# Gate logits of a routed feed-forward network: multiplied on TensorE instead of reduced on VectorE, and the instruction list written anew

## What is computed

```
x = x + (segment_sum(layernorm(x)[src] * edge_weight, dst) @ W.T + b)     # GNN
z = layernorm(x)
gates = softmax(z @ gW + gb)                   # gW is 256 x 4, gb has 4 numbers
topv, topi = top_k(gates, 2);  topw = softmax(topv)
x = x + mlp_shared(z) + sum over the 2 chosen experts of topw * mlp_expert(z)
```

## Time and profile before

| what | value |
|---|---|
| median of 3 runs | 400.21 us (397.77, 400.21, 401.97) |
| profiled execution: its own time | 397.88 us |
| its span, first to last instruction | 395.8 us |
| TensorE busy | 356.3 us (90%) |
| VectorE busy | 279.5 us (71%) |
| GpSimd busy | 277.5 us (70%) |
| ScalarE busy | 202.2 us (51%) |

### The profile page before, as it was taken

How to read it: one execution, slowest core, us unless ns; L and a number is a source line. 1 busy time by engine, 2 the same in 40 slices (tenths; PEclk the granted TensorE clock), 3 DMA queues, 4 the chain that set the end, 5 groups by cost and what they waited for, 6 DMA issues and landing times.

```text
span 395.8 us, 8049 instructions
## 1 busy us (share of the span) xinstructions
PE 356.3 (90%) x2319; PEld 284.6 (72%) x2319; DVE 279.5 (71%) x1199; ACT 202.2 (51%) x551; POOL 277.5 (70%) x294
## 2 busy tenths in 40 slices
PE   5996669989869999999999999999978999998773
PEld 3785568767768788877787877787866777766562
DVE  6598999692998999628899677662199522777371
ACT  2566796482487997023959953222085321243330
POOL 7777777777777777777777777777777777776000
PEclk9999879999989999999999999999999999999999
DMA  6999549844444554434343434343433344334000
GB/s 205 375 367 339 149 101 310 223 104 108 102 107 100 122 135 98 110 107 131 102 130 104 129 102 134 104 125 104 134 95 107 106 134 133 105 100 130 14 15 25
DMA packets 53857, 53.69 MB, mean 136 GB/s; under 512 B 32522, under 2 KB 43508, under 8 KB 53684
## 3 DMA queue, kind: packets, MB, share of 16 engines
q0 software_dynamic: 13536, 36.98, 31.3%
q1 hardware_dynamic: 35220, 10.53, 11.5%
q10 hardware_dynamic: 5056, 5.64, 4.1%
HBM read 46.64 MB, written 6.48 MB: 134 GB/s over the span
## 4 chain that ended last, share of the span: by engine, by line
PE 64%; DVE 11%; SPq 10%; issue 6%; DMA 4%; ACT 3%; DVEq 0%; ACTq 0%
PE agg_ps L1220 15%; PE hid_ps L1252 14%; SPq L739 7%; PE window_ps L1153 7%; PE tok_ps L1301 5%; DMA x_sb<-in_x 4%; PE agg_ps L1189 4%; PE build_ps L1207 3%; PE hid_ps L1265 3%; PE tok_ps L1299 3%; PE hid_ps L1261 3%; DVE gate_x L1678 3%; DVE high_node L1620 2%; PE agg_ps L1207 2%; ACT h L1006 1%
## 5 line engine op out<-in xcount | busy, mean ns | idle before, releaser
L832 POOL DMA_INDIRECT rows<-normalised_rows,src_all x246 | 239.8, 975 | 75.0 <-issue 75.0
L1220 PE MATMUL agg_ps<-xn_all,dense 128*128 128x256 f32 x350 | 79.7, 381 | 0.0
L1252 PE MATMUL hid_ps<-xt,pack 128*128 128x256 f32 (+2 forms) x336 | 70.6, 356 | 5.2 <-ACT xt L987 4.9
L1220 PEld LDWEIGHTS agg_ps<-xn_all,dense 128*128 128x128 f32 x350 | 65.3, 190 | 9.6 <-ACT dense L968 0.7
L1252 PEld LDWEIGHTS hid_ps<-xt,pack 128*128 128x128 f32 x336 | 56.0, 190 | 14.8 <-issue 8.0
L918 ACT ACTIVATE low_1h<-iota,lo_f 128x128 f32<-128x128 f32 x182 | 57.5, 393 | 0.6 <-ACT xn_all L904 0.4
L1006 ACT ACTIVATE h<-hid_ps,pack 128x256 f32<-128x256 f32 (+2 forms) x84 | 32.8, 442 | 41.4 <-PE hid_ps L1252 41.3
L1620 DVE TENSOR_SCALAR high_node<-iota,hi_f,own_w 128x125 f32<-128x125 f32 x182 | 50.6, 355 | 1.9 <-PE agg_ps L1207 1.6
L816 POOL DMA_INDIRECT rows<-in_x,src_first x36 | 35.3, 981 | 11.0 <-issue 10.4
L1678 DVE CUSTOM_DVE_ANT_0 gate_x<-xn,shared 128x256 f32<-128x256 f32 x100 | 41.9, 480 | 0.3
L1153 PE MATMUL window_ps<-rows,select 128*32 128x256 f32 x564 | 36.1, 384 | 1.7 <-DVE select L1570 1.7
(11 more groups left out here) (171 smaller groups left out, 525.5 us busy)
## 6 DMA issues: line engine op xcount, KB each, us to landing
rows<-normalised_rows,src_all POOLq DMA_INDIRECT x246
x_sb<-in_x SPq DMA_DIRECT2D x6, 512.0 KB, 10.3
normalised_rows<-xn_all ACTq DMA_DIRECT2D x6, 512.0 KB
records<-in_rec SPq DMA_DIRECT2D x184, 1.5 KB
out<-y SPq DMA_DIRECT2D x10, 256.0 KB
dense<-in_x_cols ACTq DMA_DIRECT2D x4, 512.0 KB, 8.9
pack<-in_packed SPq DMA_DIRECT2D x1, 1540.5 KB, 9.4
x_sb<-in_x SPq DMA_DIRECT2D x3, 256.0 KB, 10.7
```

The costliest lines, as they stand in the source:

```text
L832: pool.indirect_dma_start(rows[:, b % RING * BATCH + pos, :], None, table[:, :], bass.IndirectOffsetOnAxis(ap=src_all[:, c:c + 1], axis=0) ...
L1220: last = pe.matmul(dense_ps[0:r, t * D:(t + 1) * D], dense[:, h, t * P:t * P + r], xn_all[:, h, :], start=(h == 0 and t == 0), stop=(h == ...
L1252: last = pe.matmul(by_half(u.hid_ps[b % 2])[:, m % 2, 0:tok], w, u.xt[:, k, 0:tok], start=(k == 0), stop=(k == KD - 1))
```

## The change

The four logits of a tile are now two matmuls (one per half of the 256 features), with the transposed rows `xt` as the stationary operand and `gate_w_sb`, 128 x 4 per half, as the moving one, into the last eight columns of the bank `mid_ps`. The new step is `gated` (`gate_products`), after `xt`. `route` begins with a new `tensor_tensor` that adds the bias and writes `logit`, and waits for `gated` instead of for the 4 reductions a tile. `gates`, `gate_x` and its semaphore are gone; `norm` no longer waits for the reductions of the unit before. The gate weights move from the broadcast tile `shared` (1284 columns, now 260) to `pack` (8 columns more).

The list is made anew: the rank tables have other numbers, the head of the plan begins about 1 us later, `bias` of dense units may not be listed before 77.5 in the planner's clock (66.0 before), G8 comes before D3, and every TensorE duration is raised by 1.2%.

```diff
-UNIT_ORDER = "G0 D0 G1 G2 D1 G3 G4 G5 D2 G6 G7 D3 G8 G9"
+UNIT_ORDER = "G0 D0 G1 G2 D1 G3 G4 G5 D2 G6 G7 G8 D3 G9"
...
-COLD_AFTER, COLD = 1.9, 3.5
+COLD_AFTER, COLD, LATELY, ISSUE = 2.2, 4.0, 4.5, 1.012
...
-            ("dve", "bias", 0.07 + 0.265 * T, lambda: needs(66.0, prior("bias", one))),
+            ("dve", "bias", 0.07 + 0.265 * T, lambda: needs(66.0 if u.kind == "G" else 77.5, prior("bias", one))),
...
-            ("dve", "norm", 0.33 * T, lambda: needs(of("std"), prior("turn", one), prior("gates", one))),
+            ("dve", "norm", 0.33 * T, lambda: needs(of("std"), prior("turn", one))),
...
+            ("pe", "gated", 0.24 * T, lambda: needs(of("xt"))),
...
-            ("dve", "gates", 1.63 * T, lambda: needs(of("norm"))),
-            ("dve", "route", 0.29, lambda: needs(of("gates"))),
+            ("dve", "route", 0.45, lambda: needs(of("gated"))),
...
+        logit_ps = u.mid_ps[:, 512 - 2 * E:512].rearrange("p (t e) -> p t e", t=2)
...
+            def gate_products(q):
+                if q == 0:
+                    pe.wait_ge(s_w, 16)
+                pe.wait_ge(s["xt"], q + 1)
+                for t in range(UNITS[q].T):
+                    for k in range(KD):
+                        last = pe.matmul(logit_ps[:, t, :], u.xt[:, k, t * P:(t + 1) * P], gate_w_sb[:, k, :],
+                                         start=(k == 0), stop=(k == KD - 1))
+                last.then_inc(s["gated"], 1)
...
-                    dve.wait_ge(s_gate_x, E * sum(other.T for other in UNITS[:q]))
...
-            def gates(q):
-                done = E * sum(other.T for other in UNITS[:q])
-                dve.wait_ge(s["xn"], q + 1)
-                for t in range(UNITS[q].T):
-                    for e in range(E):
-                        if done >= 2:
-                            dve.wait_ge(s_gate_x, done - 1)
-                        dve.tensor_tensor_reduce(
-                            out=gate_x[:, done % 2, :], in0=u.xn[:, t, :], in1=gate_w_sb[:, e, :], scale=1.0,
-                            scalar=gate_b_sb[:, e:e + 1], op0=ALU.mult, op1=ALU.add,
-                            accum_out=u.logit[:, t, e:e + 1]).then_inc(s_gate_x, 1)
-                        done += 1
...
-                dve.wait_ge(s_gate_x, E * sum(other.T for other in UNITS[:n]))
+                dve.wait_ge(s["gated"], n)
+                dve.tensor_tensor(u.logit[R], logit_ps[R], gate_b_sb.unsqueeze(1).to_broadcast([P, T, E]),
+                                  ALU.add).then_inc(s["top"], 1)
+                dve.wait_ge(s["top"], 2 * q + 1)
```

More of the change, by code:

```diff
@@ L165 @@
 STATS_BEHIND = 3
-UNIT_ORDER = "G0 D0 G1 G2 D1 G3 G4 G5 D2 G6 G7 D3 G8 G9"
-RANKS = {"open": 3, "near": 0.021, "behind": 0.82, "dve_behind": 0.6, "act_behind": 0.83, "hurry": -0.87,
-         "batch": 2.09, "rawturn": 7.95, "rawlin": -3.57, "merge": 3.07, "windows": 10.79, "built": 1.07,
-         "rowstd": 3.76, "rawxt": 4.1, "rawout": -0.66, "low": 15.13, "select": -5.08, "select_late": 8.52,
-         "place": -10.1, "records": 4.9, "onehot": 1.04, "rowstats": 3.84, "rowshifts": -2.07}
-BUILD_RANKS = (4.56, 6.32, 2.65, -9.43)
-MULT_RANKS = (0.84, -9.23, 11.58, 11.51)
+UNIT_ORDER = "G0 D0 G1 G2 D1 G3 G4 G5 D2 G6 G7 G8 D3 G9"
+RANKS = {"open": 3, "near": 0.105, "behind": 0.46, "dve_behind": 0.83, "act_behind": 1.65, "hurry": -2.49,
+         "batch": 5.25, "rawturn": 14.77, "rawlin": -17.2, "merge": 7.43, "windows": 19.55, "built": 0.44,
+         "rowstd": 15.95, "rawxt": -2.24, "rawout": 12.98, "low": 22.59, "select": 3.55,
+         "select_late": -1.3, "place": -20.25, "records": 11.53, "onehot": -3.9, "rowstats": 5.81,
+         "rowshifts": -8.25}
+BUILD_RANKS = (2.58, 16.22, -1.26, -10.69)
+MULT_RANKS = (-5.54, -8.91, 10.79, 17.88)
 GATHER_US = 1.256
-COLD_AFTER, COLD = 1.9, 3.5
+COLD_AFTER, COLD, LATELY, ISSUE = 2.2, 4.0, 4.5, 1.012
 def schedule():
     lag = {"pe": 0.25, "act": 0.16, "dve": 0.16, "sp": 2.0}
-    free = {"pe": 35.5, "act": 43.9, "dve": 45.2, "sp": 64.2}
+    free = {"pe": 36.6, "act": 44.9, "dve": 46.2, "sp": 65.0}
     order = {e: [] for e in free}
-    cold = 0.0
-    done, units, left = {("load", 0): 31.0, ("load", 1): 46.0, ("load", 2): 58.5, ("load", 3): 61.5, ("records", 0): 35.0,
-            ("select", 0): 44.9, ("place", 0): 45.1}, [], {}
+    cold, idle = 0.0, []
+    done, units, left = {("load", 0): 31.0, ("load", 1): 46.0, ("load", 2): 59.5, ("load", 3): 62.5, ("records", 0): 36.0,
+            ("select", 0): 46.0, ("place", 0): 46.2}, [], {}
     done.update({("begin", v): 28.5 for v in range(1, len(DENSE))})
-    done.update({("onehot", k): 36.3 + 1.1 * k for k in range(EARLY)})
-    done.update({("low", k): 38.2 + 1.9 * k for k in range(EARLY)})
+    done.update({("onehot", k): 37.4 + 1.1 * k for k in range(EARLY)})
+    done.update({("low", k): 39.3 + 1.9 * k for k in range(EARLY)})
     open_units = []
@@ L396, in schedule @@
         if engine == "pe":
-            if begin - free["pe"] > COLD_AFTER:
+            idle.append((begin, begin - free["pe"]))
+            if sum(gap for to, gap in idle[-12:] if to > begin - LATELY) > COLD_AFTER:
                 cold = begin + COLD
+            took *= ISSUE
             took += min(took, max(0.0, cold - begin) / 2)
@@ L519, in build @@
         owner = sb("owner", [P, E, P // 2], BF16)
-        gate_x = sb("gate_x", [P, 2, D])
         u = WorkingSet()
@@ L661, in build @@
         steps_of_unit = (
-            "x1 stats var std rstd xn turned xt top low ex total inv gate gtop "
+            "x1 stats var std rstd xn turned xt gated top low ex total inv gate gtop "
             "ahead tied tied_before glow gex order rank kept ktotal kinv parts mix_turned mixt "
@@ L742, in load_weights @@
             def load_weights():
-                sp.dma_start(shared[:, :], every.to_broadcast([P, D + E * D + E])).then_inc(s_linear, 16)
+                sp.dma_start(shared[:, :], every.to_broadcast([P, D + E])).then_inc(s_linear, 16)
                 sp.dma_start(pack[:, :], packed).then_inc(s_w, 16)
@@ L1321, in _ @@
                         turn(q)
+                    elif name == "gated":
+                        gate_products(q)
                     elif name == "l1a":
@@ L1844, in _ @@
                         normalise(q)
-                    elif name == "gates":
-                        gates(q)
                     elif name == "route":
@@ L1917 @@
         np.asarray(L0_ffn_sW1).reshape(KD, P, D).transpose(1, 0, 2), ew1, b1,
-        np.asarray(L0_ffn_sW2).reshape(KD, P, P).transpose(1, 0, 2), ew2, b2, L0_ffn_sW3, ew3, b3_laid)], axis=1)
-    every = np.concatenate([row(L0_gnn_b), row(np.asarray(L0_ffn_gW).T), row(L0_ffn_gb)], axis=1)
+        np.asarray(L0_ffn_sW2).reshape(KD, P, P).transpose(1, 0, 2), ew2, b2, L0_ffn_sW3, ew3, b3_laid,
+        np.asarray(L0_ffn_gW).reshape(KD, P, E).transpose(1, 0, 2))], axis=1)
+    every = np.concatenate([row(L0_gnn_b), row(L0_ffn_gb)], axis=1)
     laid = [x, np.asarray(x).T, *chunks(src), *chunks(dst), *chunks(nxt), *chunks(edge_weight), rec,
```

12 lines of the change are left out of this document (6 added, 6 removed).

## The result

The kernel after the change takes 397.06 us (median of 20 executions, 394.80 to 400.25), the kernel before, run on the same chip in turns with it, 400.50 us (20 executions, 396.80 to 404.32). The ratio is 0.9934, with a 95% interval of 0.9910 to 0.9959: 0.7% faster, and the forecast of 401.1 lies 4 us too high, on the wrong side of no change; the range began at 397.5.

A forecast was written before the change was run, and what follows sets the result against it. TensorE's backlog was taken to set the end, the gathers 0.9 us behind as next bound. Terms -0.2 - 0.3 + 1.4 = +0.9 gave 398.8 on the profiled execution, 401.1 on the median's scale; range 397.5 to 405.5.

The forecast's parts named there:

- the sum: Whole kernel: -0.2 - 0.3 + 1.4 = +0.9 us, 398.8 on the profiled execution, 401.1 on the median's scale.
- The products: Gate matmuls on TensorE: 0.10 us a record, 0.40 a tile, 10.0 us for 25 tiles (8.0 to 12.2).
- From G7's `turn` to batch 23: TensorE's stretch up to the last batch: 27.6 us before, less 1.95 of first layer, plus 1.6 of gating, 27.25.
- Batch 23 to the merge: From the start of batch 23 to the merge's start: 2.46 us instead of 2.73, behind `l1b`.
- G9's `l1a` behind the merge's end: Serial tail: G9's first layer starts 6.8 us after the merge instead of 5.0, +1.8, of which gating is 0.8.
- Its first layer: G9's `l1a` to `l1c` in the tail: ScalarE's relu no longer waits behind `ex` for the logits, -0.4 us.
- TensorE's position at G7's `turn`: TensorE from 80 us to that step: 7.6 us of products against 7.5 recovered, 341.1 instead of 340.96.
- The gathers take over: Rival: ScalarE's waits go too, stream 1.2 us shorter, batch 23 met at its landing; 399.2, better end 397.7; chance 0.25.
- The floor: End of GpSimd's gather stream: last transfer lands at about 367.7, 0.9 us ahead of batch 23; could sink to 366.5.
- the low end of the range: Lower bound of the forecast time: 397.5 us, from the rival on the gathers with its better end.
- The head: Start of the kernel: `bias` of D0, moved behind more work, no longer holds VectorE 3.66 us; nothing more counted.
- TensorE falls behind: Rival: products at 0.122 us a record, only half of the 7.5 us back; +6.4 us, 406.6; chance 0.25.

The follow-up runs named there:

- E12: The kernel after, with the gates of the last three units (G8, D3, G9) reduced on VectorE right behind each unit's norm; 407.15 us, ratio 1.0133.
- E5: The kernel after with D3 ahead of G8 again in the order of units; 397.64 us, ratio 0.9947.
- E4: The kernel after without the gate products on TensorE, the logits being the bias alone; 393.77 us, ratio 0.9847.
- E9: The kernel before with one number of the plan changed, the floor for the bias of dense units 77.5 instead of 66.0; 396.30 us, ratio 0.9932.
- E13: The kernel before with the transfers of the shifted rows issued ahead of pack on SyncE's queue; 397.18 us, ratio 0.9899.
- E6: The kernel after with the dense biases allowed from 66.0 on, so that the bias of D0 is early again; 400.28 us, ratio 0.9998.
- E14: E6 with the transfers of the shifted rows issued ahead of pack on SyncE's queue; 397.75 us, ratio 0.9923.
- E1: The kernel after with the list planned with before's numbers, order of units and place of the dense biases; 407.43 us, ratio 1.0166.
- E8: The kernel after with 100 reductions more on VectorE, behind each norm, into a tile that nothing reads; 424.13 us, ratio 1.0590.
- E15: The kernel after with products kept for G0 to G4, D0, D1, the other gates planned as VectorE reductions, products planned at 0.44 us a tile; 393.70 us, ratio 0.9844.

## Why the prediction was wrong

**What held, and one size.** VectorE is busy 243.5 us instead of the 279.5 of before: 36.0 us less, where I had 47.4. I had added the durations of reductions and accumulator reads, which overlap; in a row of them one starts 0.41 us after the other (356.04, 356.45 and 356.86 in E12's timeline), so that 100 hold VectorE for 41 us and not 49.8. The time that the rival below holds to be spare rests on it, the sum doesn't. The products: 0.40 us a tile assumed, 0.37 to 0.46 measured. From G7's `turn` to batch 23: 27.25 forecast, 27.6 (341.87 to 369.48). Batch 23 to the merge: 2.46 forecast, 2.41. G9's `l1a` behind the merge's end: 6.8 forecast, 6.9 (373.98 to 380.84). Its first layer runs through without ScalarE's wait, as forecast.

**The first step that failed: "TensorE's position at G7's `turn`".** I let only the waits that VectorE ended come back, 5.8 us, and kept the 5.7 of ScalarE, "whose work is unchanged". Its work is, but not what it waits for or where its steps stand. TensorE's idle time fell from 11.5 us to 2.2 (261 less 258.8), so 9.3 came back instead of 5.8. The `turn` lies at 341.87 in a profile whose head is 3.2 us late, 338.7 without that; E5, with its first `build_ps` at 40.28, has it at 338.68. Forecast was 341.1. So the step is off by 2.4 us: 3.5 more came back, and the products took some of that (19 tiles at 0.43 instead of 0.40 would be 0.6). This was the reason of my rival "The gathers take over" (ScalarE's waits go too), and that part of it was right; but the gathers did not take over, since TensorE remains behind them. TensorE was also further behind them than I thought, as the next paragraph shows.

**The floor was misread.** I took the transfer that ends at 367.7 for the last gather. The DMA engines are idle from 366 to 367. In the trace the queue of the gathers ends at 365.6, and what moves from 367.0 on is in another queue:

```profile
366.00:367.00 1.00, 1.00 (x12) 1.00 (x11) 0.83 (x5) 0.22 (x1) 0.00 (x0) 1.00 0.00 0
367.00:367.75 0.75, 0.75 (x8) 0.68 (x7) 0.60 (x4) 0.54 (x3) 0.00 (x0) 1.00 0.50 175
```

The last gather starts at 363.3, and with the 2.9 us of E4 its rows are there at about 366.2. So TensorE was 2.4 us behind the gathers and not 0.9, and had that much more to win. In the kernel after the last gather starts at 359.7, 3.6 us earlier, where I had said within 1.5 of 363.3, and its stream is shorter by 3.6 us of busy time instead of at most 1.2. The sum doesn't use the floor, but the rival's price and the low end of the range do.

**The second step that failed: "The head", and with it the scale.** I saw that the bias would wait for nothing, and counted "nothing more". The trace of before was then put on the median's scale by adding its 2.3 us. But E9 and E13 show that the early bias is what lifts before's median: without the wait the kernel takes 396.3 to 397.2, and its executions lie within 3 to 4 us instead of 7 to 9. (More executions spread further; but the standard deviation too is 1.0 to 1.1 us in E9 and E13, and 1.7 to 2.1 for the kernel before in the same rounds.) The profile of before had been one of the quick executions. So a part of the offset of 2.3 us was no constant of the measurement but went with the wait.

**The end of the span.** From G9's `l1a` to the end the kernel after takes 15.8 us (380.84 to 396.6), that before 17.4 (378.41 to 395.8), where I had taken off 0.4. Of the 1.6 us, 0.6 come before the last addition ends (391.07 and 392.86), and 1.0 after it, in the last stores. The latter is scatter: in E5, E6 and E14, whose last unit has the same code as in the kernel after, the stretch takes 15.5, 16.9 and 17.1 us.

**The sum again.** On the scale of one execution the forecast was 398.8. Less 2.4 for the `turn`, plus 0.35 up to batch 23, less 1.2 for the end, it is 395.5; the profiled execution, 398.72 less its late head of 3.2, is 395.5 too. The median of 397.06 lies 1.5 above that, where I had added 2.3, which makes the other 0.8 of the 4.0 us. Only the 2.4 are seen in a second profile (E5). The 1.2 and the 0.8 rest on one execution of each kernel, and the split between them is no better than the scatter of a microsecond.

**The rivals.** "TensorE falls behind" was right for the gates without the new list (E1: 1.0166, near its 406.6), and wrong for the whole. The reason that I gave against it, 50 us to spare on VectorE, does not hold: E1 has that time to spare too, and in E8 the same reductions, back on VectorE at places that the plan did not give them, cost 26 us. The better end of "The gathers take over", 397.7, lies near the measured time by luck: batch 23 was not met at its landing (369.48 against some 362.6). A change of less than 1% had 0.61 and came, on the other side than forecast.

**What stays open.** How the wait costs 2.5 to 3.8 us in the median when the profiles show 0.7 to 1.9 was not seen: each kernel has one profiled execution. That the shifted rows land later still in the longer executions is a guess. The mean granted clock, which is on record for every execution, points to a second way. Of the 29 executions of the kernel before that were timed with E9, the nine shortest (397.2 us on average) have a clock of 0.977, the nine longest (402.0) one of 0.962. In E9 itself the four shortest have 0.973 and the four longest 0.977. So the long executions of the kernel before are those in which the clock is lower for longer, as in E6 against E14; whether the wait brings that about, no run shows. Nor is it known why the load of x landed late in the profile of after.

## What to carry to other kernels

A wait for a transfer in the middle of an in-order queue can cost more in the median than one profile shows; issue that transfer ahead of a large one that nobody needs yet, and look at the spread of the times as well as at their median. Before a landing is taken as a floor, make sure whose transfer it is: a kernel in which TensorE waits for it (E4) gives the time from the start of the gather to its rows. When a change comes with a new order, time the order and the change apart, and every single number of the order that touches a wait: here one number of the plan carried the net gain. A step that is moved to another engine needs its true duration in the plan and a planned place in that engine's list: put behind `norm` unplanned, the reductions cost more than they freed (E12), planned they gained (E15).
